# Tokens back in place by scatters inside the block loop instead of gathers behind it, with the first two blocks fetched together

## The chip, the cores and the metric

The kernel runs on one core of one Trainium2 chip. The metric is the device time of one execution in microseconds (us), taken as the median of several runs. The engines are PE (TensorE, matmul), PEld (its weight loads), DVE (VectorE), ACT (ScalarE), POOL (GpSimd) and SP (SyncE, which here only issues DMAs). They run their own instruction lists and meet at semaphores.

## The reference

A stack of twelve layers works on x, 2048 tokens (4 x 512) of 128 features. Each layer adds to x what a function of the normalized x gives. The tenth and the twelfth are the expert FFN that this case is about. Each token goes to one of eight experts, the one with the highest router logit, and through three small layers of that expert:

```
x = hidden_states.reshape(-1, d)
router_logits = x @ Wr + br
expert_mask = one_hot(argmax(router_logits, axis=-1), num_experts)
out = zeros_like(x)
for e in range(num_experts):
    h = gelu(x @ W1[e] + b1[e])        # 128 -> 512
    h = gelu(h @ W2[e] + b2[e])        # 512 -> 256
    y = h @ W3[e] + b3[e]              # 256 -> 128
    out = out + expert_mask[:, e:e + 1] * y
...
x = x + 0.5 * _L3_ffn_ref(_layernorm(x), ...)
```

The expert FFN is stage 9 of 0 to 11, then comes an attention layer (stage 10), then the same expert FFN with the same weights (stage 11), which ends the program with the store of x.

## The kernel before

The function `l3_ffn` (L1758) builds both expert FFNs. x stays in on-chip memory as 16 tiles of 128 tokens. The work has four parts.

**Sorting.** DVE turns the logits into a mask and computes for each token its slot in an order by expert (L1909 to L1929). Each expert's part is padded to whole blocks of 256 slots; at most 15 blocks (`NTL`) are needed, 3840 slots. POOL then scatters the normalized rows, one indirect DMA for each of the 16 tiles of tokens, to `sorted_x` in DRAM (L1986).

**Fetching a block.** From block 2 on, SP loads the block from `sorted_x` (`load_g`, L2024) when all 16 scatters have landed, and PE transposes it (L184, in `fetch`). Blocks 0 and 1 (`EARLY` = 2) don't wait for DRAM: DVE writes 16 one-hot matrices (`hot`, L1938) and PE multiplies the rows with them (L1812, L1813). SP loads the weights of each block's expert (`load_w`, L2014 to L2018) into a ring of four buffers. ACT and DVE split block and weights into a high and a low part (L1867 to L1872, L1941 to L1946).

**Computing.** `up` (128 to 512 features, four groups of three matmuls, gelu on ACT, split of the result on DVE at L1955 and L1957), `down` (512 to 256) and `last` (L1844, with the bias added on DVE at L1964, which writes y). The order of these on PE is the list `steps`, written out by hand; ACT and DVE go through the same list. Before, it is fetch 0, up 0, fetch 1, down 0, up 1, fetch 2, last 0, and then for each block down, up of the next, fetch of the one after, last.

**Back to the tokens.** SP stores y of each block to `sorted_y` (L2034, two buffers). When the last two stores have landed, POOL gathers the rows of each tile of tokens from there by `slot` (L1991, 16 indirect DMAs), and DVE adds half of each tile to x (L1977), in four chunks of four tiles. After each chunk the functions `finish_dve`, `finish_pool` and so on begin the normalization for the next stage: statistics (L201, L205) on DVE, the root on POOL (L218, L219), the normalized rows on DVE one chunk later (L240). In the last stage SP stores each chunk of x (L300).

Each engine works through its list in order. `q.wait_ge` waits on a semaphore; `tick` counts up by one at the end of an instruction and `land` when a DMA has landed.

## Time and profile before

| what | us |
|---|---|
| median of 3 runs (1895.61 to 1898.09) | 1896.71 |
| the profiled execution, its own time | 1913.12 |
| its span in the trace | 1911.3 |
| PE busy | 1556.6 (81%) |
| DVE busy | 1252.6 (66%) |
| ACT busy | 1019.6 (53%) |
| POOL busy | 599.3 (31%) |

The two expert FFNs lie at about 1321 to 1474 us and 1761 to 1911 us of the span. All times in the text are us from the start of the span. A row of a timeline gives start, duration, engine, line, operation, output<-input and shape, and in brackets how long the engine had been idle and what ended it. "issue" is idle time for which the profile shows no releaser; "remote" is a release by a semaphore for which it shows no instruction. The granted clock of PE (PEclk) is a share of 2.4 GHz, so 0.50 is 1.2 GHz. The profiled execution is 16.41 us longer than the median of the runs.

### The profile page before, as it was taken

To read this page: it belongs to the slowest core of one execution; us is meant where nothing else is said; L and a number is where in the kernel's file an instruction comes from. 1 tells how busy PE (TensorE), PEld (TensorE's weight loads), DVE (VectorE), ACT (ScalarE), POOL (GpSimd) and SP (SyncE) were. 2 spreads that over 40 slices of the span, in tenths; PEclk is the share of its full clock that TensorE was granted. 3 is DMA by queue.
4 is the path that set the end of the run, shared out by engine and by line. 5 is a ranking of instruction groups with operands and counts; after the bars stand their busy time and mean duration, and the time that the engine had idled before them with its cause. 6 is when DMAs were issued, how large, how long until landed. Compare 5 with 4: busy or idle time off the path is not lost.

```text
span 1911.3 us, 25621 instructions
## 1 busy us (share of the span) xinstructions
PE 1556.6 (81%) x9076; PEld 1066.0 (56%) x9076; DVE 1252.6 (66%) x2947; ACT 1019.6 (53%) x1832; POOL 599.3 (31%) x593
## 2 busy tenths in 40 slices
PE   4997499998799699839989976986793699995793
PEld 3776133333577488527879865985792222223693
DVE  5688488884688633563435946594683688874683
ACT  2553177787454355344537633753571378883472
POOL 3674200001387300252026637663105100002303
PEclk9999589999799799869989977997896689997797
DMA  4210804300221200110000010001561723300472
GB/s 149 60 53 12 151 17 51 50 1 1 75 72 33 67 1 1 62 45 1 1 1 11 1 45 1 1 1 51 151 202 36 163 44 51 50 1 1 151 220 83
DMA packets 113702, 103.64 MB, mean 54 GB/s; under 512 B 17654, under 2 KB 98630, under 8 KB 113352
## 3 DMA queue, kind: packets, MB, share of 16 engines
q1 hardware_dynamic: 110734, 97.02, 20.9%
q0 software_dynamic: 2048, 4.20, 0.7%
q8 instruction: 72, 1.18, 0.3%
q10 hardware_dynamic: 792, 0.79, 0.2%
q14 instruction: 56, 0.46, 0.1%
HBM read 88.21 MB, written 13.76 MB: 53 GB/s over the span
## 4 chain that ended last, share of the span: by engine, by line
PE 48%; DVE 28%; POOL 8%; ACT 6%; issue 5%; DMA 3%; POOLq 1%; SPq 0%; DVEq 0%; another core or an unknown queue 0%; ACTq 0%
PE bank L93 9%; PE bank L95 8%; PE bank L94 8%; DVE mx L2513 5%; DVE x L1494 5%; PE bank L2298 4%; PE bank L2343 4%; PE bank L2328 4%; DVE xn L240 2%; ACT e L2443 2%; DVE st L201 2%; DVE q L709 1%; POOL yg L1991 1%; PE bank L955 1%; POOL hid L796 1%
## 5 line engine op out<-in xcount | busy, mean ns | idle before, releaser
L2513 DVE TENSOR_REDUCE mx<-bank 128x1 f32<-128x512 f32 (+1 forms) x512 | 317.9, 680 | 69.8 <-PE bank L2298 69.7
L2443 ACT ACTIVATE e<-bank 128x512 f32<-128x512 f32 x512 | 266.8, 602 | 63.8 <-PE bank L2328 63.2
L2328 PE MATMUL bank<-qq,kk 99*128 99x512 bf16 (+1 forms) x512 | 164.1, 396 | 5.3 <-ACT e L2443 5.3
L2580 POOL TENSOR_TENSOR osb<-ot,rc 128x128 f32<-128x128 f32 x32 | 14.0, 436 | 443.1 <-DVE rc L2538 443.1
L1510 POOL TENSOR_TENSOR midl<-mid,midh 128x512 fp32r<-128x512 f32 (+1 forms) x96 | 126.3, 1324 | 77.5 <-ACT midh L1430 77.4
L1035 DVE TENSOR_TENSOR hl<-q,hh 128x512 fp32r<-128x512 f32 x64 | 49.1, 767 | 130.8 <-ACT hh L1005 108.8
L2328 PEld LDWEIGHTS bank<-qq,kk 99*128 99x128 bf16 (+1 forms) x512 | 40.0, 98 | 161.0 <-ACT e L2443 131.3
L184 PE MATMUL bank<-cf,xn 128*128 128x128 f32 x192 | 41.8, 358 | 99.7 <-DVE xn L240 76.1
L93 PE MATMUL bank<-wdh,midh 128*128 128x256 f32 (+1 forms) x384 | 113.2, 295 | 9.8 <-DVE x L1494 9.7
L218 POOL TENSOR_SCALAR rs<-mv 128x4 f32<-128x4 f32 x48 | 11.8, 247 | 341.7 <-DVE mv L205 340.8
L2298 PE MATMUL bank<-qq,kk 72*128 72x512 bf16 x256 | 92.2, 421 | 30.3 <-DMA qq<-scratch 20.3
L94 PE MATMUL bank<-wdl,midh 128*128 128x256 f32 (+1 forms) x384 | 110.9, 289 | 0.0
L2427 ACT CAST qq<-bank 3x512 bf16<-3x512 f32 (+1 forms) x128 | 74.0, 578 | 68.9 <-PE bank L2305 65.0
L95 PE MATMUL bank<-wdh,midl 128*128 128x256 f32 (+1 forms) x384 | 110.6, 288 | 0.0
L2298 PE MATMUL bank<-kk,qq 72*128 72x512 bf16 x256 | 93.5, 422 | 15.6 <-DMA kk<-scratch 13.2
L261 ACT COPY xT<-bank 128x512 f32<-128x512 f32 x44 | 25.6, 583 | 146.0 <-PE bank L184 146.0
L95 PE MATMUL bank<-hh,h_l 128*128 128x512 f32 x256 | 100.6, 393 | 0.0
L1425 ACT ACTIVATE mid<-bank,bu 128x512 f32<-128x512 f32 (+1 forms) x96 | 66.0, 687 | 63.4 <-PE bank L95 56.7
L1991 POOL DMA_INDIRECT yg<-sorted_y,slot x32 | 30.9, 964 | 199.9 <-DMA sorted_y<-y 191.0
L610 ACT ACTIVATE q<-bank 128x512 f32<-128x512 f32 x96 | 57.3, 597 | 65.7 <-PE bank L95 64.0
L1494 DVE SCALAR_TENSOR_TENSOR x<-ysb,gate,x 128x128 f32<-128x128 f32 x176 | 89.6, 584 | 0.1
L184 PEld LDWEIGHTS bank<-cf,xn 128*128 128x128 f32 x192 | 28.7, 183 | 109.2 <-issue 54.6
(399 smaller groups left out, 4666.1 us busy)
## 6 DMA issues: line engine op xcount, KB each, us to landing
w<-in_L_ffn_W SPq DMA_DIRECT2D x30, 512.0 KB
w<-in_L_ffn_W SPq DMA_DIRECT2D x30, 256.0 KB
qq<-scratch SPq DMA_DIRECT2D x19, 384.0 KB
w<-in_L_ffn_w_kernel SPq DMA_DIRECT2D x16, 344.0 KB
w<-in_L_ffn_w_kernel SPq DMA_DIRECT2D x16, 320.0 KB
wo<-in_L_ffn_wo_kernel SPq DMA_DIRECT2D x16, 320.0 KB
w<-in_L_ffn_W SPq DMA_DIRECT2D x30, 128.0 KB
sorted_y<-y SPq DMA_DIRECT2D x30, 128.0 KB, 1.9
```

The costliest lines, as they stand in the source:

```text
L93: e.matmul(o, l[0], r[0], start=start, stop=False)
L94: e.matmul(o, l[0], r[1], start=False, stop=False)
L95: return e.matmul(o, l[1], r[0], start=False, stop=stop)
L184: return e.transpose(o, i, ident[0:p, 0:p] if i.dtype == F32 else identb[0:p, 0:p])
L1494: e.scalar_tensor_tensor(x[:, t, :], y[:, h * 128:h * 128 + 128], gate[:, t, 2 * g + h:2 * g + h + 1], x[:, t, :], ALU.mult, ALU.add).then ...
L1510: e.tensor_tensor(l[0:fn, o], mid[i % 2][0:fn, o], h[0:fn, o].bitcast(F32), ALU.subtract).then_inc(*l2_m_lo.tick(n, i, f))
L2298: e.matmul(p, l[:, qt * 128:(qt + 1) * 128], r, start=True, stop=True).then_inc(*at_a.tick(n, t, u, j))
L2328: e.matmul(b_bank(t, u, j), keys(kk[0:K], t, b)[:, k * 128:(k + 1) * 128], queries(qq[0:K], t, b), start=True, stop=True).then_inc(*at_b.t ...
L2343: a = e.matmul(bank[6][32 * b:32 * b + (32 if kind == 0 else 9), :], lv, er[half * 4 + b][:, j * 512:(j + 1) * 512], start=(k == 0), stop= ...
L2427: e.copy(queries(pieces[(t // 4) % 2][0][96:K], t, b), i_).then_inc(*at_mrow.tick(n, t, b))
L2443: e.activation(er[u][:, j * 512:(j + 1) * 512], b_bank(t, u, j), ACT.Exp, bias=0.0, scale=scale).then_inc(*at_e.tick(n, t, u, j))
L2513: e.tensor_reduce(mxa[t % 3][:, o:o + nkb], bank[place_a["a", t, u, j]].rearrange("p (k n) -> p k n", k=nkb), X, ALU.max).then_inc(*at_max ...
```

## The change

The gathers at the end go. In their place y of each block is scattered by POOL straight to the tokens' rows of a new DRAM tensor `token_y`, two indirect DMAs of 128 rows for each block, inside the block loop. That needs for each slot the number of its token: POOL scatters the token numbers (`tokens`, 16 indirect DMAs of 128 words) to an `owners` tensor, at places that DVE works out (`places`, five instructions), and SP loads them back as `owner`. Slots without a token keep a number of a spare row behind the 2048. When the last scatter has landed, SP loads `token_y` in four plain transfers of 256 KB. The ring of y buffers grows from 2 to 5. Blocks 0 and 1 are fetched together: both sets of one-hots are written first, then both blocks are split, and only then comes up 0. ACT splits the weights of these two before their rows, and loads its gelu table with a dummy activation. The four instructions that add y to x in a chunk become one. At the program's start SP also loads `tokens` and fills the two `owners` tensors. The pieces of the diff below are, in turn, the list of steps, the lists of ACT (two pieces), DVE (three), POOL and SP.

```
-            steps = [("fetch", 0), ("up", 0), ("fetch", 1)]
-            for i in range(NTL):
+            steps = [("fetch", 0), ("fetch", 1), ("up", 0), ("up", 1), ("down", 0), ("fetch", 2), ("last", 0)]
+            for i in range(1, NTL):
                 steps += [("down", i)] + [("up", i + 1)] * (i + 1 < NTL) + [("fetch", i + 2)] * (i + 2 < NTL) + [("last", i)]
...
+                def fetch(i):
+                    if i < EARLY:
+                        weights(i)
+                    else:
+                        q.wait_ge(*up_done.at(n, i - 2, 3))
...
+                q.wait_ge(*pre_in[n % 2].at(n))
+                e.activation(gelu_table, wrb[:, 0:1], ACT.Gelu, bias=0.0, scale=1.0)
...
+                def places():
+
+                    chain(e.tensor_scalar(half, slf, 2.0 ** -7, None, ALU.mult))
+                    chain(e.tensor_tensor(cmp30, half.unsqueeze(2).to_broadcast([128, NT, 30]),
+                                          iota[:, 1:31].unsqueeze(1).to_broadcast([128, NT, 30]), ALU.is_ge))
+                    e.tensor_reduce(half, cmp30, X, ALU.add)
+                    chain(e.tensor_scalar(s30, slf, 30.0, None, ALU.mult))
+                    e.scalar_tensor_tensor(where, half, -3839.0, s30, ALU.mult, ALU.add).then_inc(*slot_set.tick(n, "place"))
...
                 def last(i):
-                    if i >= 2:
-                        q.wait_ge(*y_land[i % 2].at(n, i - 2))
+                    if i >= RING:
+                        q.wait_ge(*y_land[i % RING].at(n, i - RING))
...
                 for c in range(CHUNKS):
+                    xc, yc = (z[:, 4 * c:4 * c + 4, :].rearrange("p t n -> p (t n)") for z in (x, yg))
                     q.wait_ge(*y_back[c].at(n))
-                    for t in range(4 * c, 4 * c + 4):
-                        a = e.scalar_tensor_tensor(x[:, t, :], yg[:, t, :], 0.5, x[:, t, :], ALU.mult, ALU.add)
-                    a.then_inc(*xsum.tick(m, c))
+                    e.scalar_tensor_tensor(xc, yc, 0.5, xc, ALU.mult, ALU.add).then_inc(*xsum.tick(m, c))
...
+                q.wait_ge(*slot_set.at(n, "place"))
+                for t in range(NT):
+                    e.indirect_dma_start(ids, bass.IndirectOffsetOnAxis(ap=where[:, t:t + 1], axis=0), tokens[:, t:t + 1],
+                                         None).then_inc(*ids_in.land(n))
+                q.wait_ge(*owner_in.at(n, "owner"))
+                for i in range(NTL):
+                    q.wait_ge(*l3_y.at(n, i, 0))
+                    for h in range(2):
+                        e.indirect_dma_start(Yd, bass.IndirectOffsetOnAxis(ap=owner[:, 2 * i + h:2 * i + h + 1], axis=0),
+                                             yr[i % RING][:, h, :], None).then_inc(*y_land[i % RING].land(n, i))
...
-                    q.wait_ge(*l3_y.at(n, i, 0))
-                    e.dma_start(Y2[i], yr[i % 2]).then_inc(*y_land[i % 2].land(n, i))
                     if i + 4 < NTL:
                         load_w(i + 4)
+                    if i == 1:
+                        q.wait_ge(*ids_in.at(n))
+                        e.dma_start(owner, ids.rearrange("(p j) o -> p (j o)", p=128)).then_inc(*owner_in.land(n, "owner"))
                 nxt.sp(q)
+                for i in range(NTL - RING, NTL):
+                    q.wait_ge(*y_land[i % RING].at(n, i))
+                for c in range(CHUNKS):
+                    e.dma_start(yg[:, 4 * c:4 * c + 4, :],
+                                Yd[0:2048].rearrange("(t p) n -> p t n", p=128)[:, 4 * c:4 * c + 4, :]).then_inc(*y_back[c].land(n))
```

On DVE, around the second set of one-hots of the first FFN (`hot_454` is the set of block 0 and `hot_455` that of block 1; `xxl`, `w1l`, `w2l` are the low parts of rows and weights, `hh` and `hl` the split of up 0), the order before was:

```order
1333 L1957 TENSOR_TENSOR hl_444<-q_449,hh_443 128x256 [waits l3_h_hi]
1334 L1955 CAST hh_443<-q_447 128x256 [waits gelu_set]
1335 L1957 TENSOR_TENSOR hl_444<-q_447,hh_443 128x256 [waits l3_h_hi]
1336 L1936 TENSOR_SCALAR here_428<-slf_427 128x16 [waits one_hot]
1337 L1938 TENSOR_SCALAR hot_455<-cf,here_428 128x256 [waits dve_step]
1338 L1938 TENSOR_SCALAR hot_455<-cf,here_428 128x256 x15
1339 L1941 TENSOR_TENSOR xxl_442<-bank,xxh_441 128x256 [waits x_hi]
1340 L1944 TENSOR_TENSOR w1l_416<-w_396,w1h_415 128x512 [waits w_hi]
1341 L1946 TENSOR_TENSOR w2l_418<-w_397,w2h_417 128x1024 [waits w_hi]
```

And in the changed kernel, where `hot_463` and `hot_464` are the sets of blocks 0 and 1:

```order
1323 L1951 TENSOR_SCALAR hot_463<-cf,here_428 128x256 [waits dve_step]
1324 L1951 TENSOR_SCALAR hot_463<-cf,here_428 128x256 x15
1325 L1949 TENSOR_SCALAR here_428<-slf_427 128x16 [waits one_hot]
1326 L1951 TENSOR_SCALAR hot_464<-cf,here_428 128x256 [waits dve_step]
1327 L1951 TENSOR_SCALAR hot_464<-cf,here_428 128x256 x15
1328 L1965 TENSOR_TENSOR xxl_446<-bank,xxh_445 128x256 [waits x_hi]
1329 L1968 TENSOR_TENSOR w1l_412<-w_391,w1h_411 128x512 [waits w_hi]
1330 L1970 TENSOR_TENSOR w2l_414<-w_392,w2h_413 128x1024 [waits w_hi]
1331 L1965 TENSOR_TENSOR xxl_448<-bank,xxh_447 128x256 [waits x_hi]
1332 L1968 TENSOR_TENSOR w1l_416<-w_396,w1h_415 128x512 [waits w_hi]
1333 L1970 TENSOR_TENSOR w2l_418<-w_397,w2h_417 128x1024 [waits w_hi]
1334 L1979 CAST hh_449<-q_453 128x256 [waits gelu_set]
```

The second set has moved from behind the whole of up 0 to directly behind the first, and the split of block 1 now also stands ahead of up 0's.

On POOL, from the scatters of the first FFN on (`slot` holds the tokens' slots, `yg` the gathered rows), the order before was:

```order
442 L1986 DMA sorted_x<-xn,slot_435 3840x128 [waits slot_set,zero_in,stage_end]
443 L1986 DMA sorted_x<-xn,slot_435 3840x128 x15
444 L1991 DMA yg_456<-sorted_y,slot_435 128x128 [waits y_land1,y_land0]
445 L1991 DMA yg_456<-sorted_y,slot_435 128x128 x7
446 L218 TENSOR_SCALAR rs<-mv 128x4 [waits var]
447 L219 TENSOR_TENSOR rs<-rs,cf 128x4 [waits pool_step]
448 L1991 DMA yg_456<-sorted_y,slot_435 128x128 x4
449 L218 TENSOR_SCALAR rs<-mv 128x4 [waits var]
```

And in the changed kernel (`where` holds the places of the token numbers, `owner` the token numbers by slot, and `x_in0` is the semaphore of the load of `owner`):

```order
442 L2013 DMA sorted_x<-xn,slot_435 3840x128 [waits slot_set,zero_in,stage_end]
443 L2013 DMA sorted_x<-xn,slot_435 3840x128 x15
444 L2018 DMA owners<-tokens,where_436 3840x1 [waits slot_set]
445 L2018 DMA owners<-tokens,where_436 3840x1 x15
446 L2024 DMA token_y<-y_458,owner_441 5888x128 [waits l3_y,x_in0]
447 L2024 DMA token_y<-y_458,owner_441 5888x128
448 L2024 DMA token_y<-y_459,owner_441 5888x128 [waits l3_y]
449 L2024 DMA token_y<-y_459,owner_441 5888x128
```

The gathers, which waited for the last two stores, have gone; 16 scatters of token numbers and two scatters for each of 15 blocks stand in their place, and the roots (L218, L219) come after all of them.

## Rows read from the trace of the kernel before

**Rows 1.** The page: a costliest group (busy, mean ns, idle before); a DMA issue (KB, us)
```profile
L1991 POOL DMA_INDIRECT yg<-sorted_y,slot x32 | 30.9, 964 | 199.9 <-DMA sorted_y<-y 191.0
...
sorted_y<-y SPq DMA_DIRECT2D x30, 128.0 KB, 1.9
```

**Rows 2.** Timeline, DVE, end of the first FFN: start, length, instruction, idle before
```profile
1441.69 0.42 DVE L1964 TENSOR_TENSOR y<-bank,b 128x256 f32<-128x256 f32 x1 [3.39 <-PE bank L1844]
...
1450.49 0.96 DVE L1977 SCALAR_TENSOR_TENSOR x<-yg,x 128x128 f32<-128x128 f32 x4 [8.37 <-DMA yg<-sorted_y,slot]
...
1468.45 0.90 DVE L1977 SCALAR_TENSOR_TENSOR x<-yg,x 128x128 f32<-128x128 f32 x4 [3.42 <-DMA yg<-sorted_y,slot]
...
1470.29 0.86 DVE L201 BATCH_NORM_STATS2 st<-x 128x6 f32<-128x128 f32 x4
...
1471.19 0.38 DVE L205 BATCH_NORM_AGGREGATE mv<-st 128x2 f32<-128x6 f32 x4
...
1473.04 1.12 DVE L240 TENSOR_SCALAR xn<-x,mv,rs 128x128 f32<-128x128 f32 x4 [1.48 <-POOL rs L219]
```

**Rows 3.** Timeline, POOL, the first and the last of 16 gathers, first FFN
```profile
1444.22 0.99 POOL L1991 DMA_INDIRECT yg<-sorted_y,slot  x1 [94.66 <-DMA sorted_y<-y]
...
1465.99 0.95 POOL L1991 DMA_INDIRECT yg<-sorted_y,slot  x1 [0.30 <-issue]
```

**Rows 4.** Timeline, end of the second FFN and of the program
```profile
1883.01 0.42 DVE L1964 TENSOR_TENSOR y<-bank,b 128x256 f32<-128x256 f32 x1 [3.40 <-PE bank L1844]
...
1905.22 0.94 POOL L1991 DMA_INDIRECT yg<-sorted_y,slot  x1 [0.31 <-issue]
...
1907.68 0.90 DVE L1977 SCALAR_TENSOR_TENSOR x<-yg,x 128x128 f32<-128x128 f32 x4 [4.23 <-DMA yg<-sorted_y,slot]
```

**Rows 5.** DMA view: issues of 1 MB and of 256 KB (KB each, us to landing)
```profile
h<-in_h1T SPq DMA_DIRECT2D x2, 1024.0 KB, 8.0
...
w<-in_w1T SPq DMA_DIRECT2D x2, 256.0 KB, 2.7
```

**Rows 6.** Source view of L184 (features of a sorted block), first FFN, then second
```profile
L184 PE MATMUL bank<-cf,g x26: 270/272/273, 1359.9 to 1429.7; 128*128 128x128 f32 x26
...
L184 PE MATMUL bank<-cf,g x26: 270/273/273, 1800.8 to 1871.0; 128*128 128x128 f32 x26
```

**Rows 7.** Tile views: scatters of both FFNs, of the first; landing of block loads
```profile
L1986 POOL DMA_INDIRECT sorted_x<-xn,slot x32: 957/962/1698, 1329.1 to 1788.9; - x32
...
L1986 POOL DMA_INDIRECT sorted_x<-xn,slot x16: 957/962/1325, 1329.1 to 1348.6; - x16
...
DMA to landing us min/median/max: 1.9/1.9/1.9
```

**Rows 8.** Timeline, SP queue: the first load of sorted blocks, first FFN, then second
```profile
1351.85 0.92 SPq L2024 DMA_DIRECT2D g<-sorted_x  x3
...
1791.22 1.41 SPq L2024 DMA_DIRECT2D g<-sorted_x  x3
```

**Rows 9.** Timeline, DVE, first FFN: the two sets of 16 one-hots
```profile
1328.39 4.87 DVE L1938 TENSOR_SCALAR hot<-cf,here 128x256 fp32r<-128x256 f32 x16
...
1349.17 4.41 DVE L1938 TENSOR_SCALAR hot<-cf,here 128x256 fp32r<-128x256 f32 x16
```

**Rows 10.** Waits, 1320 to 1372 us: who waited for whom, total, times, longest
```profile
ACT q L1879 <- remote: 6.2, 2, 3.1
```

**Rows 11.** Windows of 2 us: busy (count) of PE, PEld, DVE, ACT, POOL; PEclk, DMA, GB/s
```profile
1350.00:1352.00 2.00, 2.00 (x10) 2.00 (x10) 2.00 (x9) 0.00 (x0) 0.00 (x0) 0.50 0.15 46
...
1356.00:1358.00 2.00, 2.00 (x19) 2.00 (x18) 1.39 (x3) 2.00 (x4) 0.00 (x0) 1.00 0.00 0
...
1778.00:1780.00 2.00, 0.18 (x1) 0.19 (x2) 1.25 (x3) 1.91 (x4) 1.69 (x2) 0.50 1.12 331
```

**Rows 12.** Program start: DMA view on the fill's landing; timeline, DVE, first stage
```profile
sorted_x<-zeros SPq DMA_DIRECT2D x1, 1920.0 KB, 11.0
...
30.46 0.28 DVE L666 TENSOR_REDUCE mx<-lg 128x16 f32<-128x128 f32 x1 [5.98 <-POOLq L341]
```

More of the change, by code:

```diff
@@ L1769, in l3_ffn @@
             n8, cum, n8b = take("n8", 8), take("cum", 8), take("n8b", 8)
-            slot = take("slot", 16).bitcast(U32)
+            slot, where = take("slot", 16).bitcast(U32), take("where", 16).bitcast(U32)
+            half, s30, gelu_table = take("half", 16), take("s30", 16), take("gelu", 1)
+            cmp30 = take("cmp30", 16 * 30).rearrange("p (t k) -> p t k", k=30)
+            owner = take("owner", 2 * NTL).bitcast(U32)
             gr = [take("g", 256).rearrange("p (h n) -> p h n", h=2) for _ in range(3)]
@@ L1775, in l3_ffn @@
             h2r = [take("h2", 512).rearrange("p (k n) -> p k n", k=2) for _ in range(2)]
-            yr = [take("y", 256).rearrange("p (h n) -> p h n", h=2) for _ in range(2)]
+            yr = [take("y", 256).rearrange("p (h n) -> p h n", h=2) for _ in range(RING)]
             hot = [take("hot", 16 * 256, F32R) for _ in range(EARLY)]
@@ L1861, in act, with weights @@
                 e = q.e
-                def fetch(i):
-                    if i >= 2:
-                        q.wait_ge(*up_done.at(n, i - 2, 3))
-                    q.wait_ge(*dispatched.at(n, i))
-                    e.copy(xr[i % 2][0], place["fetch", i, 0][:, 0:256]).then_inc(*x_hi.tick(n, i))
+                def weights(i):
                     q.wait_ge(*ex_load[i % 4].at(n, i))
@@ L1872, in fetch @@
                     e.copy(wh[i % 2][1][0], wb[i % 4][1].rearrange("p k n -> p (k n)")).then_inc(*w_hi.tick(n, i, 2))
+                def fetch(i):
[3 more added lines that the diff above has]
+                        q.wait_ge(*up_done.at(n, i - 2, 3))
+                    q.wait_ge(*dispatched.at(n, i))
+                    e.copy(xr[i % 2][0], place["fetch", i, 0][:, 0:256]).then_inc(*x_hi.tick(n, i))
+                    if i >= EARLY:
+                        weights(i)
                 def up(i):
@@ L1971, in dve @@
                         up(i)
+                        if i == 0:
+                            places()
                     elif s == "last":
@@ L2781, in sp_program @@
             first_pre.sp(q)
+            e.dma_start(tokens[:, :], ins["token_ids"]).then_inc(*zero_in.land())
+            for o in ("owners0", "owners1"):
+                e.dma_start(*(z.rearrange("(p j) o -> p (j o)", p=128) for z in (ins[o], ins["spare_rows"]))).then_inc(*zero_in.land())
             q.wait_ge(*zero_in.at())
```

48 lines of the change are left out of this document (23 added, 25 removed).

## The prediction

> **What bounds the kernel now.** I read the page first: PE is busy for 81% of the span, so only stretches where it stands still can give much. POOL's gathers are 30.9 us of work, and before them POOL waited 191.0 us for the stores of y [rows 1]; that wait costs nothing by itself, but it says that all 16 gathers of an FFN stand behind its last block. The timeline of the end of the first FFN shows it from DVE: its last y ends at 1442.11, then DVE waits for gathers, and the normalized rows of the last chunk end at 1474.16, 32.0 us later [rows 2]. POOL issues a gather every 1.27 us or so from 1444.22 to 1466.94, and that row is the path [rows 3]. The second FFN ends in the same way: last y at 1883.43, last sum into x at 1908.58, 25.2 us later [rows 4]. The third view is the start of an FFN. Block 2 is transposed at 1359.9 and 1800.8 [rows 6], and its load is issued at 1351.85 and 1791.22 [rows 8]. So two things end late there: PE and DVE work for blocks 0 and 1, in which the second set of one-hots begins only at 1349.17 though the first was done at 1333.26 [rows 9]; and, some 6 to 8 us before that work is through, the scatter to DRAM with the load behind it. A fetch costs as before once the loop runs: from block 2 to 14 in 69.8 us, 5.8 us a block [rows 6].
>
> **End of the first FFN.** T is the end of the last y. Removed are the store, landing 1.9 us after its issue [rows 1], and 16 gathers. Added on the path: POOL sees y (0.26 us, as between the landed store and 1444.22, estimated), then two scatters, 0.98 + 0.30 + 0.96 [rows 3]: T + 2.5. Their landing is not in the trace for this tensor. The nearest rows are the row scatters: the last one of the first FFN ends at 1349.56 and SP goes on at 1351.85, 2.3 us [rows 7, 8]; in the second 1789.9 and 1791.22, 1.3 us. I take 1.8: T + 4.3. Then a load of 256 KB: 2.7 us [rows 5], with 1.9 for 128 KB as the lower end [rows 7]: T + 7.0. From there DVE sets the pace. Chunk 0: one sum over 512 columns (four now take 0.90 [rows 2]; I take 0.8), 0.86 and 0.38 of statistics: T + 9.0. Each further chunk waits 1.48 us for POOL's root (its sum lies in that wait), then 1.12 + 0.86 + 0.38 [rows 2]: 3.84 us, three times, and at last 1.48 + 1.12. That is T + 23.1, for 32.0 before: **8.9 us less**. The three later loads are hidden, as they have 3.84 us each.
>
> **End of the second.** There is no normalization behind it, so the last of the four loads counts. A single transfer of 1 MB took 8.0 us and one of 256 KB 2.7 us [rows 5]. Four together lie between; I take 6.5 (nearer to 8.0, since rows of 512 bytes are moved): T + 10.8, the sum 0.8: T + 11.6, for 25.2 before [rows 4]. The store of the last chunk is the same. **13.6 us less.**
>
> **Start of both FFNs.** The second set of one-hots now follows the first: about 4.9 us after 1333.3 it is done. The 32 matmuls of fetch 1 no longer stand between up 0 and down 0. PE then has up 0, up 1 and down 0 to do and next needs block 2. That load can't move: POOL issues 16 scatters as before, and the load lands 1.9 us after issue at best [rows 7], so at 1353.75 and about 1793.2. Against 1359.9 and 1800.8 this gives at most 6.2 + 7.6 = 13.8 us. Three things are to be taken off. First, up 0 stands under an odd delay: ACT twice waited 3.1 us for a release of matmuls that the trace shows as done [rows 10], while SP's loads of four blocks of weights, and the scatters, were under way (the last of these loads was issued just ahead of 1351.85). If that comes again, it lasts until then, and the split of up 0 and down 0 still follow: I put fetch 2 at 2.4 us after the load, 4.8 us in both, with 0 and 10 as ends. Second, PE now stands still ahead of block 2. In 1778 to 1780, where it did one matmul, its granted clock was 0.50 (1.2 GHz); in 1350 to 1352, just after its wait for the second one-hots, it did 10 matmuls at that clock, and 19 in 2 us at 2.4 GHz later [rows 11]. If 4 us of the loop's first work run so, 2 us are lost in each, 4.0 in both, ends 0 and 6. Third, POOL now works beside DVE in the loop. The one-hots took 4.87 us while POOL scattered and 4.41 us without [rows 9]: a tenth more. DVE is nearly as loaded as PE in a block, and POOL will be at work in 2.5 of 5.8 us. Half of a tenth of that on the path over 13 blocks is about 1.6 us: 3.0 in both, ends 0 and 8. What is left is 13.8 - 4.8 - 4.0 - 3.0 = **2.0 us less**.
>
> The Trainium skill bears on this third point ("SBUF — State Buffer", section "SBUF: two separate sides"): GpSimd and certain DVE instructions take one pair of ports in turn, and whoever comes second waits for the whole instruction. Its section "A bandwidth-pool intuition that's wrong (but worth ruling out)" gives a POOL-issued DMA 3.1 us beside a DVE copy, for 0.62 alone. The rows here agree with a small wait only; what the large one would do is the last rival.
>
> **Costs put at nothing.** The five instructions of `places` are small and lie in DVE's wait for block 2; without that cover they would cost about 2 us in each FFN. The gelu table's load moves into ACT's idle time. Token numbers: 16 scatters of 128 words, at 1.27 us as the row scatters (same count of descriptors; ends 1.0 and 2.0), run from 1349.9 to 1370.2, landed at 1372.5. SP stands there from about 1363 on, and behind it wait the load of block 6, its weights, and all later ones. Block 6 is needed at about 1377 + 5.8, and its load takes 1.9 us alone [rows 7] and, as an estimate, up to twice that beside loads of weights; so 5 us or more of slack cover it, and if they are used up, each further us is paid once in each FFN. POOL starts on y three blocks late, but needs 2.5 us where a block takes 5.8, and catches up at block 5; the ring of five holds that. The three transfers at the program's start follow a fill that lands 11.0 us after its issue, with the first stage beginning at 30.46 [rows 12].
>
> **Sum.** 8.9 + 13.6 + 2.0 = 24.5 us less, against the profiled execution's 1913.12 (span 1911.3 and 1.8 around it): 1888.6. The median is 16.4 us below that execution, and I take the same difference there: 1896.7 - 24.5 = **1872.2 us**.
>
> **Rivals.**
> - The delays of up 0 belong to the profiled execution alone. For it: they and PE's standing still behind them make up some 16 us, about what that execution has over the median. Against it: nothing shows where that excess lies. Then fetch 2 already stood at the load in the timed runs, the starts give nothing, and the two deductions of clock and POOL stay in part or in full: 22.5 - 0 to 7, so 1874 to 1881, middle 1878.
> - The starts give all that the load allows: 22.5 + 10 to 13.8, so 1861 to 1865. For it: DVE and PE have 14 us from the second set of one-hots to the load. Against: [rows 10, 11].
> - The token numbers land late (2.0 us a scatter instead of 1.27 adds 12 us, 7 beyond the slack): 14 us dearer, 1886. Against: 962 ns is the median of 32 scatters.
> - Slower: POOL's scatters of y fall behind in the loop. It decides from 2.9 us a scatter on, when two need more than a block's 5.8 us. At 3.4 us a block needs 6.8: 15 of them from 1374 on end at 1476, against T at 1440, so 36 us later, less the 22.5 and 2 of gains over both FFNs: 2 x 36 - 24.5, about 47 us slower, 1944. Against: the longest of 32 scatters took 1.70 us, with DVE at work beside many of them [rows 7]. By the skill's 3.1 us, an estimate from that page, one would come near this; no row here does.
>
> **How the numbers follow.** The forecast (1867 to 1875) has 0.45, the first rival 0.30, the full start 0.10, late numbers 0.06, POOL falling behind 0.04; 0.05 is for landing times of scatters and loads at their far ends (2.3 instead of 1.8 in both FFNs and 8.0 instead of 6.5 in the second: 2.5 us dearer). The range is 1863 to 1883. About 0.2% (3.8 us) is what a measurement of this kernel can tell from no change: faster 0.95, the same 0.01, slower 0.04.
>
> **What would show it.** The four loads of `token_y` issued about 4.3 us after the last y in both FFNs; the last normalized row of the first about 23 us after its last y, and the last sum of the second about 11.6 us after it. The first transposes of L184 at 1354 to 1357 and near 1796, with PE idle and at 0.50 ahead of them. POOL done with a block's scatters before the next y from block 5 or 6 on. The forecast is wrong if a scatter of y takes over 2 us in the loop, if PE waits for the load of block 6 or 7, if the distance from block to block grows beyond 5.9 us, or if the end of an FFN still takes more than 27 us to the next stage.

## The result and the profile after

| | us | n |
|---|---|---|
| before, median | 1896.71 (1892.40 to 1898.09) | 5 |
| changed, median | 1885.58 (1882.91 to 1889.61) | 5 |
| ratio, 95% interval | 0.9938 (0.9921 to 0.9956) | |
| changed, profiled execution | 1883.84 (span 1881.7) | 1 |

The change makes the kernel 11.1 us faster. Forecast were 24.5 us less and 1872.2 us, with 1863 to 1883 as the range: right in sign, but more than twice what was measured, and outside the range.

**Both ends came out as forecast.** Timeline of the kernel after, DVE (to answer [rows 2, 4]), first FFN and then the second:

```profile
1439.45 0.42 DVE L1988 TENSOR_TENSOR y<-bank,b 128x256 f32<-128x256 f32 x1 [3.34 <-PE bank L1850]
1446.69 0.69 DVE L2005 SCALAR_TENSOR_TENSOR x<-yg,x 128x512 f32<-128x512 f32 x1 [6.82 <-DMA yg<-token_y]
...
1450.54 1.12 DVE L240 TENSOR_SCALAR xn<-x,mv,rs 128x128 f32<-128x128 f32 x4 [1.25 <-POOL rs L219]
...
1462.57 1.12 DVE L240 TENSOR_SCALAR xn<-x,mv,rs 128x128 f32<-128x128 f32 x4 [1.47 <-POOL rs L219]
...
1867.55 0.42 DVE L1988 TENSOR_TENSOR y<-bank,b 128x256 f32<-128x256 f32 x1 [3.39 <-PE bank L1850]
1875.52 3.01 DVE L2005 SCALAR_TENSOR_TENSOR x<-yg,x 128x512 f32<-128x512 f32 x4 [7.55 <-DMA yg<-token_y]
```

From the last y (its end, 1439.87) to the last normalized row (1463.69) it is 23.8 us, where 23.1 were forecast and 32.05 stood before. In the second FFN the last sum ends 10.6 us after the last y (forecast 11.6, before 25.2). On the way there, POOL and the SP queue (to answer [rows 3]):

```profile
1440.15 0.96 POOL L2024 DMA_INDIRECT token_y<-y,owner  x1 [1.55 <-DVE y L1988]
1441.41 0.95 POOL L2024 DMA_INDIRECT token_y<-y,owner  x1 [0.30 <-issue]
```

```profile
1443.73 2.03 SPq L2069 DMA_DIRECT2D yg<-token_y  x4
```

Two scatters, and loads issued 3.9 us after y (forecast 4.3). Counted from the last y, the two ends save 8.2 us (to the last normalized row) and 14.1 (to the end of the program).

**The starts lose.** Source view of L184 in the first FFN of the kernel after (to answer [rows 6]), and the granted clock in windows behind it (columns as in [rows 11]):

```profile
L184 PE MATMUL bank<-cf,g x26: 270/272/447, 1354.4 to 1427.5; 128*128 128x128 f32 x26
its engine sat idle before it (us, times) until:
  issue: 7.9, 1
  DMA g<-sorted_x: 7.7, 1
...
1356.00:1358.00 2.00, 2.00 (x11) 2.00 (x11) 1.70 (x2) 0.96 (x2) 1.56 (x2) 0.50 0.01 0
1358.00:1360.00 2.00, 2.00 (x11) 2.00 (x10) 0.55 (x2) 0.47 (x1) 1.70 (x2) 0.50 0.02 1
1360.00:1362.00 2.00, 2.00 (x18) 2.00 (x18) 0.00 (x0) 0.79 (x3) 1.39 (x3) 0.95 0.76 218
```

PE stands still for 7.7 us, and then does 11 matmuls in 2 us instead of 18 until about 1360. A distance below is the time from the transpose of one block to that of the next; from block 2 to 3 it is 7.95 us here, 5.8 to 5.9 later in the loop. Two more things show. SP waits for the token numbers (waits of the SP queue, 1350 to 1400; 3.9 us in the second FFN), which makes the loads of block 6 and its weights late: two block distances of 6.43 and 6.26 us. And POOL's row scatters grow while DVE splits the 1024 columns of the second weights (POOL, then DVE):

```profile
SPq L2064 <- DMA owners<-tokens,where: 4.3, 1, 4.3
```

```profile
1338.70 1.96 POOL L2013 DMA_INDIRECT sorted_x<-xn,slot  x1 [0.30 <-issue]
1340.97 1.77 POOL L2013 DMA_INDIRECT sorted_x<-xn,slot  x1 [0.30 <-issue]
```

```profile
1338.62 1.21 DVE L1970 TENSOR_TENSOR w2l<-w,w2h 128x1024 fp32r<-128x1024 f32 x1
...
1340.69 1.21 DVE L1970 TENSOR_TENSOR w2l<-w,w2h 128x1024 fp32r<-128x1024 f32 x1
```

In before the two met once, in the second FFN (POOL, then DVE; it is the longest scatter of [rows 7]):

```profile
1780.30 1.70 POOL L1986 DMA_INDIRECT sorted_x<-xn,slot  x1 [0.30 <-issue]
```

```profile
1779.94 1.23 DVE L1946 TENSOR_TENSOR w2l<-w,w2h 128x1024 fp32r<-128x1024 f32 x1 [0.18 <-issue]
```

Which "before" this is to be compared with was the open question.

### The profile page after: what moved, and what is told of

It reads as the page before. It is cut to its first block, busy times and chain, and to the rows that moved or that the text cites. A ratio compares the mean times of both kernels' runs of the same rounds, so it can differ in the third digit from the quotient of the medians.

```text
span 1881.7 us, 25680 instructions
## 1 busy us (share of the span) xinstructions
PE 1558.9 (83%) x9076; PEld 1065.6 (57%) x9076; DVE 1256.9 (67%) x2933; ACT 1019.6 (54%) x1834; POOL 668.4 (36%) x653
## 3 DMA queue, kind: packets, MB, share of 16 engines
q1 hardware_dynamic: 107294, 95.25, 21.1%
## 4 chain that ended last, share of the span: by engine, by line
PE 44%; DVE 28%; POOL 11%; ACT 6%; issue 6%; DMA 4%; POOLq 1%; SPq 1%; DVEq 0%; ACTq 0%
PE bank L93 8%; PE bank L95 7%; PE bank L94 7%; DVE mx L2546 5%; DVE x L1494 5%; PE bank L2331 5%; PE bank L2376 4%; PE bank L2361 4%; DVE xn L240 2%; POOL sorted_x L2013 2%; DVE st L201 2%; ACT e L2476 2%; POOL owners L2018 2%; DVE q L709 2%; PE bank L955 1%
## 5 line engine op out<-in xcount | busy, mean ns | idle before, releaser
L1510 POOL TENSOR_TENSOR midl<-mid,midh 128x512 fp32r<-128x512 f32 (+1 forms) x96 | 131.7, 1381 | 72.6 <-ACT midh L1430 72.5
L218 POOL TENSOR_SCALAR rs<-mv 128x4 f32<-128x4 f32 x48 | 12.7, 265 | 347.7 <-DVE mv L205 346.9
L184 PE MATMUL bank<-cf,xn 128*128 128x128 f32 x192 | 42.2, 361 | 89.6 <-DVE xn L240 65.9
L2024 POOL DMA_INDIRECT token_y<-y,owner x60 | 59.3, 988 | 79.8 <-DVE y L1988 59.8
L709 DVE TENSOR_TENSOR q<-q,bank 128x512 f32<-128x512 f32 x96 | 63.8, 683 | 33.0 <-ACT q L610 32.0
```

What stands on the lines that cost most here:

```text
L709: e.tensor_tensor(v, v, up_bank(i, f)[1] if f < 5 else up_bank(i, f)[0][64:112, :], ALU.mult).then_inc(*mul_set.tick(n, i, f))
L1510: e.tensor_tensor(l[0:fn, o], mid[i % 2][0:fn, o], h[0:fn, o].bitcast(F32), ALU.subtract).then_inc(*l2_m_lo.tick(n, i, f))
```

## The experiments

Times are set against runs of before on the same chip, made between them. Each group ran on a chip of its own, and the level of before differs between groups. The ratio is not the quotient of the two medians, and it differs from it by 0.001 at most.

| group | before, median | kernel | median | ratio (95%) |
|---|---|---|---|---|
| 1 | 1896.69 | before_again | 1897.17 | 1.0006 (0.9993 to 1.0020) |
| 1 | | fetch_only | 1904.79 | 1.0038 (1.0023 to 1.0052) |
| 1 | | scatter_only | 1887.97 | 0.9947 (0.9931 to 0.9964) |
| 1 | | warm | 1887.97 | 0.9950 (0.9934 to 0.9966) |
| 2 | 1913.30 | after_again | 1920.44 | 1.0026 (1.0008 to 1.0043) |
| 2 | | late_full | 1935.34 | 1.0118 (1.0088 to 1.0148) |
| 2 | | late_scatter | 1957.51 | 1.0224 (1.0198 to 1.0251) |
| 2 | | no_ids | 1904.89 | 0.9952 (0.9935 to 0.9969) |
| 3 | 1917.47 | after_third | 1927.55 | 1.0054 (1.0035 to 1.0073) |
| 3 | | row_words | 1905.41 | 0.9935 (0.9920 to 0.9950) |
| 3 | | row_full | 1896.35 | 0.9889 (0.9871 to 0.9907) |
| 3 | | before_ids | 1959.79 | 1.0215 (1.0200 to 1.0231) |
| 4 | 1915.73 | row_full_2 | 1896.45 | 0.9910 (0.9895 to 0.9925) |
| 4 | | row_words_2 | 1901.20 | 0.9917 (0.9901 to 0.9934) |
| 4 | | before_ids_2 | 1951.46 | 1.0192 (1.0177 to 1.0207) |
| 4 | | plain_ids | 1926.48 | 1.0049 (1.0032 to 1.0067) |
| 5 | 1913.95 | row_full_3 | 1896.95 | 0.9912 (0.9895 to 0.9928) |
| 5 | | before_ids_3 | 1955.80 | 1.0221 (1.0204 to 1.0239) |

### Group 1: the parts alone

**before_again** is the kernel before, for a trace from the chip of this group.

> The kernel before, unchanged, for a second trace of it. Theory A (the trace I predicted from was of an unusual execution: its late releases of up 0 belong to it alone): span near 1892 to 1897, ACT waits for no release over 1 us at the start of an FFN, and block 2 is transposed about 1 us or less behind the landing of its load, some 30.5 to 33 us after the mask (in the first trace 37.1 and 38.2). Theory B (the late releases are the rule, and the gain went elsewhere): block 2 again 36 to 38 us after the mask. Ratio to the kernel before 1.000 by both.

Its L184, first FFN (to answer [rows 6] again):

```profile
L184 PE MATMUL bank<-cf,g x26: 270/272/301, 1351.3 to 1420.8; 128*128 128x128 f32 x26
its engine sat idle before it (us, times) until:
  ACT q L1879: 0.3, 1
```

Block 2 is transposed 30.1 us after the cast of the mask that opens the FFN (29.9 in the second); in the trace that the prediction was made from it was 37.1 and 38.2. Its last scatter of rows ends at 26.7, and the transpose begins 3.4 us later. So block 2 waits for nothing but its load, and the stretch that fetching together was to free is not there. Nor does any engine wait for a "remote" release in this trace; before's first trace has [rows 10].

**fetch_only** has the new order at the start alone; y is stored and gathered as before.

```diff
-steps = [("fetch", 0), ("up", 0), ("fetch", 1)]
+steps = [("fetch", 0), ("fetch", 1), ("up", 0), ("up", 1), ("down", 0), ("fetch", 2), ("last", 0)]
... (and the lists of ACT and DVE as in the change)
```

> Blocks 0 and 1 fetched together, with the gelu table early, but y stored and gathered as before. Theory A: no gain or a loss of 1 to 6 us against the kernel before, since block 2 waits for its load anyway and PE comes out of the wait at 1.2 GHz (about 2.5 us in each FFN). Theory B: 5 to 12 us faster than the kernel before.

It is 8.1 us slower than before's runs and 7.6 slower than before_again's. By the traces the last y stands 5.3 and 3.2 us later after the mask than in before_again. So this half of the change costs time here, by itself.

**scatter_only** is the changed kernel with the old order (the same diff, reversed).

> The scatters in the loop and the merged sums, but blocks 0 and 1 fetched as before. Theory A: 16 to 21 us faster than the kernel before, so faster than the full change by 4 to 8 us. Theory B: the ends give less in timed runs than in the trace; 8 to 12 us faster than the kernel before, and slower than or equal to the full change.

8.7 us faster. SP's wait for the numbers stands out now, since PE comes to block 6 sooner:

```profile
SPq L2053 <- DMA owners<-tokens,where: 6.6, 1, 6.6
```

One block distance of 9.1 us in the first FFN and one of 7.1 us in the second (instead of 5.8) go to it. The gain is less than the 16 to 21 us of theory A; by the time, theory B was the nearer. The two halves do not add up to the whole, either: 8.1 us lost and 8.7 won, against 11.1 won by the whole in its own runs. By the traces each half puts the last y later (fetch_only by 8.5 us over both FFNs, scatter_only by 7.4), but the whole only by 9.2, since a later block 2 covers part of SP's wait. The rest of the difference stays open.

**warm** is the changed kernel with 50 matmuls, whose result is overwritten, ahead of PE's wait for block 2.

```diff
+if i == EARLY:
+    for r in range(50):
+        e.matmul(p[:, 0:256], xh[0][:, 0:128], hot[0][:, 0:256], start=True, stop=True)
 q.wait_ge(*g_load[i % 3].at(n, i))
```

> The changed kernel with 50 further matmuls of 256 columns on PE ahead of the wait for block 2 (into the bank that the transposes overwrite), 5.9 us at 2.4 GHz, so that PE does not stand still for more than 3 us there. Theory A: PE leaves the wait at 2.4 GHz, the distance from the first to the second fetch of a sorted block falls from 7.95 and 6.95 us to 5.8, and the time by 3 to 5 us against the changed kernel (1880 to 1883). A rival, that the clock costs nothing because the loop has slack: no difference.

The distance from block 2 to 3 falls from 7.95 and 6.95 us to 5.28 and 5.26, and the granted clock is 1.00 from 1354 to 1364 us, where the changed kernel had 0.50; so what the distance had above was the clock after standing still. The two distances at SP's wait in the first FFN grow to 7.0 and 6.2. By the traces 2.1 and 1.8 us are won up to the last y; the timed gain over before, 8.7 us, does not show them.

### Group 2: another chip

**after_again** is the changed kernel. **late_full** and **late_scatter** are the changed kernel and scatter_only with SP's wait for the numbers two blocks later.

```diff
-if i == 1:
+if i == 3:
     q.wait_ge(*ids_in.at(n))
     e.dma_start(owner, ...)
```

**no_ids** leaves out the 16 scatters of token numbers in each FFN and SP's wait for them, so that the rows of y go to rows by slot and not by token.

```diff
-q.wait_ge(*slot_set.at(n, "place"))
-for t in range(NT):
-    e.indirect_dma_start(ids, ..., tokens[:, t:t + 1], None).then_inc(*ids_in.land(n))
...
-q.wait_ge(*ids_in.at(n))
```

> The changed kernel, unchanged, for a second trace and as the measure for the three beside it. Theory A (the loss against a usual execution of the kernel before is made of three parts: row scatters lengthened beside DVE's splits, PE's clock after the wait for block 2, SP's wait for the token numbers): last y 115 to 118 us after the mask in both FFNs, first block distances 7.0 to 8.0 us, one distance at the fifth sorted block over 6.2 us in the first FFN. If the first trace was chance, these spread by more than 2 us.

> The changed kernel with SP's wait for the token numbers, and the load of owner, two blocks later (at block 3 in place of block 1), so that the loads of blocks 6 and 7 stand ahead of it. Theory A: the long distances at the fifth and sixth sorted block (6.43, 6.26 us) fall to 5.8, last y 1.1 us earlier in the first FFN and 0.2 in the second: 1 us faster than the changed kernel at most. Rival (the stall is hidden anyway, and the distances come from POOL's scatters): distances unchanged.

> Scatters in the loop with blocks 0 and 1 fetched as before, and SP's wait for the token numbers at block 3. In scatter_only that wait made one distance 9.06 us and 7.1 us. Theory A: both fall to 5.9, last y 112.5 to 113.5 us after the mask in both FFNs, and the time 4 to 6 us below scatter_only and 2 to 4 below the changed kernel: 1881 to 1884, the best of all. Rival (the wait only moves, and the ring of y buffers or POOL's backlog holds the loop instead): a long distance again, at a later block.

> The changed kernel without the 32 scatters of token numbers and without SP's wait for them; owner is loaded from the tensor as filled at the start, so y rows go to rows in order of slots and not to the tokens. Theory A: no long distance but the first, last y 1.1 and 0.2 us earlier than in the changed kernel, and nothing more: 1 to 2 us faster. Rival (the token numbers' small writes or POOL's work beside DVE slow the whole loop): every distance shorter by 0.1 us or more and 3 to 6 us faster.

Little came as expected. The last y of after_again comes 130.6 and 131.1 us after the mask, not 115 to 118. In late_full the fifth and sixth distance do fall to 5.8 to 5.9, as by theory A, but in each FFN a second one of 15 to 17 us comes up, from block 9 to 10, and it is 14.9 us slower than after_again; late_scatter, expected to be the best, is 44.2 us slower than before. Only no_ids gains: 8.4 us against before, 15.6 against after_again, where 1 to 2 or 3 to 6 were expected. Before itself takes 1913.3 us here, as its first profiled execution did (1913.12), and the changed kernel is slower than it. Waits of after_again, 1336 to 1395 us:

```profile
ACT xxh L1882 <- remote: 14.4, 3, 13.2
...
DVE xxl L1965 <- ACT xxh L1882: 11.9, 1, 11.9
```

Here the distance from block 4 to 5 is 15.3 us, and 15.8 in the second FFN. By the trace PE had done its matmuls long before and gone on to others; what came late was the semaphore. I paired each PE instruction that raises a semaphore with the next event of that semaphore in the trace that belongs to no other instruction:

| trace | group | PE's releases over 0.4 us late | the longest, us | waits on "remote", us |
|---|---|---|---|---|
| before (first) | | 7 | 8.1 | 29.3 |
| after (first) | | 0 | | 0 |
| before_again, fetch_only, scatter_only, warm | 1 | 0 in each | | 0 |
| after_again | 2 | 54 | 13.0 | 35.2 |
| no_ids | 2 | 37 | 12.9 | 37.7 |
| after_third | 3 | 57 | 14.6 | 56.9 |
| row_full | 3 | 20 | 13.1 | 30.4 |
| before_ids | 3 | 24 | 13.8 | 61.1 |
| plain_ids | 4 | 8 | 10.8 | 39.0 |

All late ones lie inside the two FFNs. Releases by ACT and DVE come 0.01 us after the instruction (a few in 2000 pair with a later one), and so do PE's outside the FFNs. Where PE's are late, up to 5 per cent of the three engines' events are missing from the trace, so counts and longest times depend on the pairing by a few; the zeros don't. SP shows the same stretches: in before's first trace its issues of weight loads, 0.5 to 0.6 us apart otherwise, stand 1.4 us apart while POOL scatters rows:

```profile
1336.24 0.02 SPq L2015 DMA_DIRECT2D w<-in_L_ffn_W  x1
1337.68 0.00 SPq L2016 DMA_DIRECT2D w<-in_L_ffn_W  x1
1339.13 0.00 SPq L2017 DMA_DIRECT2D bc<-in_b12c  x1
```

So chips differ: on some of them (groups 2 to 5, and the chip of before's first profile) PE's releases are held back in the FFNs, on others (group 1 and the runs that the prediction was measured by) never. Where they are held back, before is at 1913 to 1917 us, else at 1897. (The kind goes with the group; whether it is the chip or something else that a group shares, these runs can't tell.)

In late_full the second stall begins when POOL works off the stored-up scatters of y in one go (ACT, then POOL with the last of 14 in a row):

```profile
1416.49 0.47 ACT L1899 ACTIVATE h<-bank,bc 128x256 f32<-128x256 f32 x1 [5.92 <-remote]
1419.37 1.20 ACT L1891 ACTIVATE q<-bank,bc 128x256 f32<-128x256 f32 x3 [2.41 <-remote]
```

```profile
1398.92 0.96 POOL L2024 DMA_INDIRECT token_y<-y,owner  x1 [19.92 <-DMA owner<-owners]
...
1416.59 0.96 POOL L2024 DMA_INDIRECT token_y<-y,owner  x1 [0.30 <-issue]
```

In no_ids it is the 10 scatters of y from 1377.42 to 1391.08: five releases come singly between 1382.4 and 1388.4, up to 3.0 us late, and the other six together at 1392.0 to 1392.3. It is so in the other traces too: while a train runs, releases come one by one, 0.7 us and more apart, and where some are still held at its end, these come 0.05 us apart soon after it. (In before's first trace the three late ones of the first FFN come at 1340.56, 1344.10 and 1347.63, all before the train's end at 1349.56.) That gave the theory of the next group: a train of scatters holds PE's releases back.

### Group 3: the theory, and a kernel from it

> The changed kernel once more, as the yardstick of this group of runs. So far it was 11.1 us faster than before on one chip and 7.1 us slower on another, where the traces show PE's semaphore releases up to 13 us late while POOL issues scatters. Theory: there are two kinds of chip, and the ratio follows the kind: near 0.994 where no release of PE is late, near 1.003 where they are. Rival: the ratio drifts from hour to hour and has nothing to do with late releases; then a ratio of 0.994 comes with late releases in the trace, or one of 1.003 without.

As group 2: 54 and 57 late releases, slower than before both times.

**before_ids** is the kernel before with the instructions of `places` and a second train of 16 scatters, for which nothing waits until the gathers at the end.

```diff
+q.wait_ge(*slot_set.at(n, "place"))
+for t in range(NT):
+    e.indirect_dma_start(ids, bass.IndirectOffsetOnAxis(ap=where[:, t:t + 1], axis=0), tokens[:, t:t + 1],
+                         None).then_inc(*ids_in.land(n))
 def gather(c):
```

> The kernel before, plus the five instructions that compute places and the 16 scatters of token numbers behind the row scatters, for which nothing waits until the gathers at the end. Theory of late releases: on a chip without them, 0 to 3 us more than before; on a chip with them the second train of scatters holds back PE's semaphore updates in the loop as in the changed kernel, and one block distance in each FFN grows by 8 to 15 us: 16 to 30 us slower than before. Rival: what stalls is SP's wait for the numbers; SP has no such wait here, so it costs nothing on either kind of chip.

42.3 us slower, more than expected. Timeline of its ACT, its POOL and its windows (columns as in [rows 11]):

```profile
1374.04 0.47 ACT L1892 ACTIVATE h<-bank,bc 128x256 f32<-128x256 f32 x1 [5.26 <-remote]
1382.53 0.47 ACT L1892 ACTIVATE h<-bank,bc 128x256 f32<-128x256 f32 x1 [8.02 <-remote]
```

```profile
1359.73 1.03 POOL L2007 DMA_INDIRECT owners<-tokens,where  x1 [3.68 <-DVE where L1943]
...
1378.74 0.96 POOL L2007 DMA_INDIRECT owners<-tokens,where  x1 [0.30 <-issue]
```

```profile
1376.00:1384.00 8.00, 0.94 (x4) 0.94 (x5) 0.57 (x2) 1.47 (x4) 2.88 (x3) 0.50 0.01 0
```

In these 8 us hardly anything computes, and DMA is at 0.01. The last scatter ends at 1379.70, and six releases, up to 13.8 us old, come between 1382.5 and 1382.8. Nothing in the loop waits for the train, so SP's wait for the numbers is not what stalls here. The block distance at this place is 20.2 us in the first FFN and 19.5 in the second, 28 us more than twice 5.9. Of the other 14 us, some 10.5 lie ahead of block 2, which comes 40.9 and 44.8 us after the mask, against 37.1 and 38.2 in before's first trace (of another chip; there is none of this one). They are of the kind that plain_ids shows below without this train.

**row_words** gets the numbers without a train. A row of `sorted_x` has 132 words, the 129th being the token's number (or a spare row's). A block's numbers come with its load, DVE copies them (157 ns a block), and for blocks 0 and 1 SP loads them apart. POOL's copies of the rows (1.96 and 0.29 us) lie in its 7 to 8 us of waiting for the slots. `places` and SP's wait for the numbers go with the train. The order at the start is the old one. **row_full** has the new order.

```diff
+e.tensor_copy(xs[:, :, 0:128], xn[:, :, :])...
+e.tensor_copy(xs[:, :, 128:132].bitcast(U32), tokens[:, :].unsqueeze(2).to_broadcast([128, NT, 4]))...
 for t in range(NT):
-    e.indirect_dma_start(Gd, ..., xn[:, t, :], None)
+    e.indirect_dma_start(Gd, ..., xs[:, t, :], None)
-for t in range(NT):
-    e.indirect_dma_start(ids, ..., tokens[:, t:t + 1], None).then_inc(*ids_in.land(n))
...
+e.tensor_copy(owner[:, 2 * i:2 * i + 2].unsqueeze(2), gr[i % 3][:, :, 128:129].bitcast(U32))...
```

> The changed kernel with the order of before at the start (fetch 0, up 0, fetch 1) and without the 16 scatters of token numbers: the number rides in a 129th word of each scattered row, and DVE copies a block's numbers from the loaded block (one instruction of about 0.1 us a block). SP waits for nothing of POOL's in the loop. Theory: what is left is the shorter ends (about 8.5 and 14 us) and nothing is paid in the loop: 1874 to 1878 on a chip without late releases (20 us less than before), and about 20 us less than before on a chip with them too, since only the 16 scatters of rows that before has as well stand in a train. Rival: the time lost belongs to the y scatters in the loop, which are all kept; then it stays near the changed kernel with the old order, 8 to 10 us less than before on a chip without late releases.

> As row_words, but with the changed kernel's order at the start (both first blocks fetched together). Theory: the order costs what it cost alone, where it made the kernel 7.6 us slower: 4 to 8 us above row_words. Rival, as the prediction had it: the old order's price shows only where POOL and SP are busy, and without the numbers' scatters fetching together gives up to 2 us: row_full is at or below row_words.

row_full is 21.1 us faster than before and 31.2 us faster than the changed kernel on this chip; row_words is 12.1 us faster than before, where about 20 were expected. The steady distance is 5.87 us in both, no block stands out, and POOL scatters y in pairs from block 0 on:

```profile
1370.85 0.95 POOL L2016 DMA_INDIRECT token_y<-y,first  x1 [15.18 <-DVE y L1981]
1372.11 1.11 POOL L2016 DMA_INDIRECT token_y<-y,first  x1 [0.30 <-issue]
1377.18 0.96 POOL L2016 DMA_INDIRECT token_y<-y,first  x1 [3.96 <-DVE y L1981]
```

The expectation on the order fell: here row_words is 9.1 us behind row_full. On such a chip PE's releases are late through the train of row scatters, and in the old order the second set of one-hots and fetch 1 come only behind the late ones. Its longest wait of ACT on "remote" is 28.0 us, against 12.6 in row_full.

### Groups 4 and 5: repeats, and what kind of DMA

> row_full once more, in the hope of the other kind of chip. With late releases it was 21.1 us faster than before and 9.1 us faster than row_words. Theory: on a chip without late releases the start of before has nothing to give, so fetching together costs its 4 to 8 us and row_full lies above row_words, about 1878 to 1884 against before's 1897. On a chip with late releases: again about 21 us less than before. Rival: fetching together gains on every chip once the numbers' scatters are gone; then row_full is the faster of the two here as well.

> row_words once more. Theory: without late releases it is the fastest of all, 1874 to 1878, and 4 to 8 us below row_full. With late releases again 12 us less than before. Rival: as with row_full_2, it stays above row_full.

> before_ids once more: the second train of scatters with nobody waiting for it. With late releases it was 42 us slower than before. Theory: without them 0 to 3 us slower; with them again about 40. Rival: the train itself costs by its DMA traffic or its use of POOL and SBUF, whatever the chip: then 20 us or more on this chip too, with no release of PE late.

> row_full a third time. With late releases (two chips) it was 21.1 and 17 to 19 us faster than before. Theory, for a chip without late releases: the ends give 22 us, fetching together takes back its 8 or 9 us less what the missing numbers' scatters save: 1880 to 1885 against 1897. With late releases: 1895 to 1897 against 1914 to 1917 once more.

> before_ids a third time. With late releases (two chips) it was 42 and 36 us slower than before. Theory, for a chip without them: 0 to 3 us slower. Rival: the train costs on every chip: 20 us or more. With late releases: 36 to 42 us slower once more.

All fell on chips with late releases: row_full 19.3 and 17.0 us faster than before, before_ids 35.7 and 41.9 us slower. row_words_2 is 14.5 us faster than before, and row_full_2 leads it by 4.8 us. What row_full, row_words and before_ids cost on a chip of group 1's kind, no run shows.

**plain_ids** is before_ids with plain DMAs of the same 128 words.

```diff
-    e.indirect_dma_start(ids, bass.IndirectOffsetOnAxis(ap=where[:, t:t + 1], axis=0), tokens[:, t:t + 1],
-                         None).then_inc(*ids_in.land(n))
+    e.dma_start(ids[128 * t:128 * t + 128], tokens[:, t:t + 1]).then_inc(*ids_in.land(n))
```

> before_ids with the 16 scatters by address replaced by 16 plain DMAs that POOL issues, of the same 128 words each, to consecutive places. It tells what holds back PE's releases on a chip where they are late. Theory: it is POOL issuing a train of DMAs, since each writes descriptors as a scatter does: again 8 us and more late, 20 to 45 us slower than before. Rival: only scatters by an address list do it (POOL reads the list and builds 128 descriptors by itself): no release is late beyond those of the row scatters, 0 to 3 us slower. Without late releases on this chip it tells nothing of the two, and costs 0 to 3 us.

Tile view of its `owners`:

```profile
L2007 POOL DMA_DIRECT2D owners<-tokens x32: 537/538/600, 1361.6 to 1817.5; - x32
```

All of its 8 late releases were held beside the row scatters, none beside the new train, and the block distances are 5.8 to 5.9 us throughout. Against before_ids_2 on the same chip that is 25.0 us less. So POOL issuing DMAs is not enough. That it is the addressing is the likely reading but not shown alone: this train is also shorter (8.6 us instead of 20) and writes to consecutive places, and only four releases of PE fall into its two stretches, all 0.01 us after their instruction.

The kernel is still 10.8 us slower than before, more than the rival's 0 to 3. Its trace tells where: block 2 comes 43.4 and 43.2 us after the mask, 6.3 and 5.0 later than in before's first trace (of another chip). 1.75 us of each are the five instructions of `places`, which stand in DVE's list directly ahead of the second set of one-hots:

```profile
1359.43 0.17 DVE L1938 TENSOR_SCALAR half<-slf 128x16 f32<-128x16 f32 x1
...
1361.18 0.17 DVE L1950 TENSOR_SCALAR here<-slf 128x16 f32<-128x16 f32 x1
```

The rest stands ahead of them, with releases of up 0 held longer beside the row scatters (10.8 us at most instead of 8.1). Why longer stays open; before has no trace from this chip.

## Why the prediction was wrong

- **End of the first FFN (8.9 forecast): right**, 8.2. Only the chunk was undersized: 4.13, 4.13 and 3.78 us from one L240 to the next instead of three times 3.84.
- **End of the second (13.6): right**, 14.1. The loads landed sooner than assumed, and the four sums then ran as one, 3.01 us.
- **Start of both FFNs (2.0 less): this step failed.** "Against 1359.9 and 1800.8 this gives at most 6.2 + 7.6 = 13.8 us" took 1359.9 and 1800.8 [rows 6] for the kernel's, but they were this one chip's. Where the change was measured, block 2 already stood right behind its load (before_again), 30.1 and 29.9 us after the mask instead of 37.1 and 38.2. So the 13.8 us were nothing, while most of what was deducted from them was real.
- **The changed kernel's own side of the start** was forecast well. Block 2 at 2.4 us after the load is 33.3 and 33.0 us after the mask, and it came at 32.4 and 31.0. Of the deductions PE's clock was right too (4.0 forecast; the first distance is 2.5 and 1.6 us above before_again's, 4.1).
- **What the starts cost in fact.** Against before_again the last y comes 5.8 and 3.4 us later after the mask. In the first FFN that is 2.25 from a later block 2 (the last row scatter ends 2.0 later, lengthened by DVE's split), 2.5 from PE's clock after the wait, and 1.1 from SP's wait for the numbers. Against before_again the ends give 8.3 and 14.6 us, so the two FFNs save 23.0 - 9.2 = 13.8 us by the traces. The spans differ by 10.2 and the timed medians by 11.1: 0.9 us ahead of the first mask and 2.7 between the two FFNs go the other way, in stretches that the change hardly touches and that differ by up to 10 and 5 us among all the traces.
- **"I take the same difference there: 1896.7 - 24.5"** is the same fault in the sum: the 16.4 us between the profiled execution and the median were not noise around it but the very stretches that the term spent. In before_again the second set of one-hots begins 7.2 and 9.1 us sooner after the mask than in before's first trace.
- **The first rival was right in kind** ("the delays of up 0 belong to the profiled execution alone") and had 0.30. It gave 1874 to 1881. Its upper end lacked the row scatters' 2.0 and 1.0 us and SP's wait. A row for the first was there: the longest scatter of [rows 7], 1.70 us, stood beside this split in the second FFN of before. "Against it: nothing shows where that excess lies" was weak: [rows 10] did show it, as a wait for matmuls already done (the two rows have 6.2 us; all waits on "remote" in that trace make 29.3).
- **"5 us or more of slack cover it"** (token numbers) was just too little: SP held 4.3 us, and 1.1 us came through in the first FFN. The prediction's own signs of being wrong, a wait for block 6 and a distance over 5.9 us, did show. The y scatters did catch up at block 5, as forecast.
- **The rival of late numbers gave 1886, next to the measured 1885.58, and that is luck:** it wanted 2.0 us a scatter and 14 us lost. The scatters of numbers took 1.3 us each (1351.09 to 1371.76), and their lateness cost 1.1 us in the first FFN and about 0.2 in the second.
- **POOL beside DVE in the loop (3.0):** too high. The steady distance stayed at 5.75 to 5.9 us and 60 scatters of y took 988 ns on average. So the last rival did not come up.
- **On the kind of chip that was profiled the sum came near for what it counted, and missed the largest term.** There row_full, which has the change without the numbers' train, the wait for it and `places`, is 17 to 21 us faster, near the 24.5. The train and what hangs on it, put at nothing, make 31 us on the one chip where both kernels ran, enough to make the changed kernel 7 to 10 us slower than before. No row of before showed a train beside the loop; but the row scatters, its only train beside PE's work, stood beside its only late releases.

## What to carry to other kernels

Look whether an engine waits for work that is already done ("remote" in the waits), and what else was under way then: such a wait can be absent on another chip, as it was in group 1. A gain worked out from a profile counts only where the timed runs have the stretch too; if the profiled execution is 16 us above them, find those 16 us first and take out every term that rests on them. A list of numbers that must be scattered can ride in the rows that are scattered anyway, as in row_full: it saves the train, and the wait for it.

## What was not expected of the hardware

- On four of the five chips of the groups (2 to 5), PE's semaphore releases were up to 17.8 us late (before_ids_2) while POOL worked through a train of 8 to 32 scatters by address: some came singly during the train, and those still held came together 1 to 4 us after its end. A pair of scatters in each block held them 0.5 to 1.4 us, at a block distance of 5.87 us all the same (row_full). ACT's and DVE's releases took 0.01 us. On group 1's chip the same kernels showed none. Why chips differ stays open.
- SP's issues are held in the same stretches: 1.4 us apart in the rows of before above, and in row_words an issue of `load_w` (L2024) stands at 1353.68 and the next (L2025) at 1356.51, where they are 0.5 us apart elsewhere. In before_again, on group 1's chip, the same issues beside the row scatters are mostly 0.5 us apart.
- A scatter of 128 rows takes up to 1.96 us instead of 0.96 when DVE begins a tensor_tensor of 1024 columns (1.21 us) beside it. Three of the longest, in after and before, lost 1.00, 0.81 and 0.74 us, when 1.13, 0.93 and 0.87 us of DVE's instruction were left at their start: the scatter waits for about what is left of it. The Trainium skill ("SBUF — State Buffer", section "SBUF: two separate sides") tells of such turns between the two; the waits of 0.7 to 1.0 us agree, and the 3.1 us of its section "A bandwidth-pool intuition that's wrong (but worth ruling out)" were seen in no run here.
